# When the second and third groups' embedding gathers may be issued in a recommendation tower on one core

## The reference

```python
e = jnp.stack([tbl_0[ids[:, 0]], ..., tbl_38[ids[:, 38]]], axis=1)      # 512 x 39 x 16
# three layers, W of 128 x (39 * fields before); each one:
Xi = einsum('hjk,bjd,bkd->bhd', W.reshape(H, 39, Fi), X0, Xi) + b
res.append(Xi.sum(axis=2))                                              # 512 x 128
z = concatenate(res, axis=1)                                            # 512 x 384
h = relu(concatenate([z, dense_ctx]) @ W_top1 + b_top1)                 # 400 -> 512
h = relu(h @ W_top2 + b_top2)                                           # 512 -> 256
y = h @ W_top3                                                          # 512 x 1
```

## Time and profile before

| what | value |
|---|---|
| median of 3 executions | 723.21 us |
| lowest and highest of the 3 | 718.61 and 725.51 us |
| the profiled execution | 719.22 us |
| its span, first to last instruction | 716.8 us |
| mean granted TensorE clock in it | 0.981 |
| busy share of the span | PE 93%, DVE 82%, ACT 78%, POOL 49% |
| indirect DMAs of the whole kernel | 160, 955 ns each on POOL |

### The profile page before, as it was taken

One profiled execution on the slowest core, in us unless ns is written; L12 is line 12 of the kernel. 1 busy time (PEld: TensorE's weight loads), 2 busy tenths in 40 slices (PEclk: granted clock), 3 DMA queues, 4 the chain that ended last, 5 costly groups with the idle time before them and its releaser, 6 DMA issues.

```text
span 716.8 us, 11884 instructions
## 1 busy us (share of the span) xinstructions
PE 666.3 (93%) x2654; PEld 473.6 (66%) x2654; DVE 590.9 (82%) x956; ACT 558.5 (78%) x1939; POOL 347.9 (49%) x382
## 2 busy tenths in 40 slices
PE   3248899999999999999999999999999999999998
PEld 3135577777676767677767776677767777766653
DVE  3134789899998999899989998999989999999940
ACT  2114788988887888789878987998798888888842
POOL 7720388283747464655656474647464414002400
PEclk9759999999999999999999999999999999999999
DMA  8100561323223141414040504141414130200000
GB/s 274 17 7 9 111 169 24 71 47 67 51 60 59 37 80 26 88 17 102 11 103 9 109 8 105 12 105 12 104 14 101 13 99 6 75 1 1 0 1 0
DMA packets 66273, 39.51 MB, mean 55 GB/s; under 512 B 57558, under 2 KB 60630, under 8 KB 64084
## 3 DMA queue, kind: packets, MB, share of 16 engines
q1 hardware_dynamic: 59343, 37.58, 23.3%
q0 software_dynamic: 5120, 1.29, 2.0%
q10 hardware_dynamic: 1760, 0.15, 0.2%
HBM read 32.66 MB, written 2.40 MB: 49 GB/s over the span
## 4 chain that ended last, share of the span: by engine, by line
PE 75%; ACT 7%; issue 6%; DVE 5%; another core or an unknown queue 3%; DMA 3%; ACTq 0%; SPq 0%; POOL 0%; DVEq 0%; POOLq 0%
PE yb L913 17%; PE yb L914 16%; PE yb L915 16%; PE p L879 12%; ACT yb L571 5%; PE pq L890 4%; DVE acc L745 3%; DMA gram<-in_L_rec_W_dram 1%; PE yb L831 1%; PE p L989 1%; PE pq L844 1%; PE yb L1007 1%; DMA late<-x_scratch 1%; PE p L985 1%
## 5 line engine op out<-in xcount | busy, mean ns | idle before, releaser
L571 ACT ACTIVATE yb<-yb,x0t 128x128 f32<-128x128 f32 x1728 | 467.1, 379 | 78.6 <-PE yb L915 70.6
L745 DVE TENSOR_TENSOR acc<-acc,yb 128x512 f32<-128x512 f32 (+1 forms) x576 | 385.4, 669 | 40.5 <-ACT yb L571 9.1
L913 PE MATMUL yb<-w1h,x1h 128*128 128x512 f32 (+1 forms) x640 | 314.8, 492 | 6.9 <-DVE acc L745 4.0
L915 PE MATMUL yb<-w1h,x1l 128*128 128x512 f32 (+1 forms) x640 | 247.8, 387 | 0.0
L914 PE MATMUL yb<-w1l,x1h 128*128 128x512 f32 (+1 forms) x640 | 247.8, 387 | 0.0
L451 POOL TENSOR_TENSOR late<-late,x0r 117x512 f32<-117x512 f32 (+1 forms) x105 | 132.1, 1292 | 110.6 <-DMA late<-x_scratch 110.4
L913 PEld LDWEIGHTS yb<-w1h,x1h 128*128 128x128 f32 x640 | 120.0, 188 | 89.6 <-DVE acc L745 54.9
L400 POOL DMA_INDIRECT emb<-in_table_dram,idx x160 | 152.8, 955 | 43.0 <-issue 40.0
L914 PEld LDWEIGHTS yb<-w1l,x1h 128*128 128x128 f32 x640 | 120.8, 189 | 41.0 <-issue 24.8
L915 PEld LDWEIGHTS yb<-w1h,x1l 128*128 128x128 f32 x640 | 120.1, 188 | 24.7
L440 POOL TENSOR_TENSOR bdiag<-mask,x0t 128x312 f32<-128x312 f32 x64 | 45.5, 710 | 161.9 <-PE pq L890 158.5
(11 more groups left out here) (84 smaller groups left out, 327.2 us busy)
## 6 DMA issues: line engine op xcount, KB each, us to landing
late<-x_scratch SPq DMA_DIRECT2D x45, 312.0 KB
late<-x_scratch SPq DMA_DIRECT2D x30, 234.0 KB
emb<-in_table_dram,idx POOLq DMA_INDIRECT x160
gram<-in_L_rec_W_dram SPq DMA_DIRECT2D x1, 2496.0 KB
x_scratch<-x0r SPq DMA_DIRECT2D x15, 156.0 KB
late<-x_scratch SPq DMA_DIRECT2D x15, 156.0 KB
w2t<-in_L_rec_W_dram SPq DMA_DIRECT2D x1, 1280.0 KB
x0t<-embt SPq DMA_DIRECT2D x64, 20.0 KB
```

Source lines behind the costliest of these rows:

```text
L571: op = act.activation(part, part, ACT.Copy, scale=x0t[u][:, t, j:j + 1])
L745: dve.tensor_tensor(part, part, parts(y_bank(t, m), n), ALU.add).then_inc(summed, 1)
L913: pe.matmul(y[:, 0:w], hi, w1h[:, at:at + w], start=True, stop=False)
L915: pe.matmul(y[:, 0:w], lo, w1h[:, at:at + w], start=False, stop=True).then_inc(bank_ready, 1)
```

## The change

In the program of POOL every gather of group 1 first waits for `w_hi`. For gather i (0 to 9) the value is 2 + 10 - 10 + i + 1 = i + 3, so the first waits for ACT's first copy of W1 (n = 2), the sixth for its sixth, and the tenth for all 12 copies. No wait is written for group 2's gathers; they stand behind the tenth in the same queue. Nothing else differs.

```diff
                 rows_of(u, u)
                 pool.wait_ge(idx_ready, 2 * (u + 1))
                 for i in range(PER_Q):
+                    if u == 1:
+                        pool.wait_ge(w_hi, W0_BANKS + W_BANKS - PER_Q + i + 1)
                     gather(u, i)
             pool.wait_ge(embq_ready, 1)
             rows_of(2, 0)
```

## The result

The changed kernel takes 717.9 us (median of 20 executions, 714.95 to 720.19), the kernel before 722.8 us beside it (20 executions). The ratio is 0.9928, with a 95% interval of 0.9913 to 0.9942: 4.9 us faster, inside the 1% that the prediction called no change, and a third of the 14.6 us forecast. The profiled execution took 714.95 us with a span of 712.8, against 719.22 and 716.8 before.

What follows compares the result with a forecast made beforehand. The prediction took the opening to be bound by ACT's copies of W1, held up by gathers delaying PE's signals. Copies 17.0 us sooner, less 2.4 for group 2's run, gave 14.6 us: 708.6 us from 723.2, range 702 to 727.

Steps and rivals of the forecast that it cites:

- What bounds the kernel: Opening: bound by ACT's copies of W1, waiting 24.1 us because a long unbroken run of gathers holds back PE's signals.
- the gathers are not the cause: Rival on the opening: PE's signal is late for another reason, no change, 723.2 us; chance 0.15.
- The copies: ACT's copies of W1: sixth begins at 25.6, last ends at 30.8 instead of 47.79, 17.0 us sooner.
- That group 1 and group 2 would be there in time: Gathered rows: group 1 there by 37, wanted at 41.6; group 2 there by 51, wanted at 58.7.
- Group 2's run beside the first layer: First layer of group 0, 36 to 48 us: group 2's ten gathers delay PE's signals, costing 2.4 us.
- the upper bound: First layer: signals held until 4.2 us after the last gather, opening ends at 61.7, leaving 3.0 us of gain.
- The prediction's own signs: Opening: waits for remote in a first-layer stage over 11.4 us show a moved stall; line 554 after 55 refutes the forecast.
- the stall moves: Rival on the first layer: group 2's run holds its signals as the weights' were held, 720.2 us; chance 0.15.
- every gather arms the stall again: Rival on the copies of W1: one gather holds each next signal about 8.4 us, 735.1 us; chance 0.16, including otherwise slower.

Runs made afterwards that it cites:

- e1: The changed kernel without group 2's ten gathers in the opening (group 2 computed from group 0's rows): 703.0 us, 0.972 of the kernel before.
- e17: The changed kernel itself, unaltered, timed a third time in the fifth session: 717.3 us against 720.3 for the kernel before, 0.996.
- e3: The changed kernel with all ten gathers of group 1 waiting for the last of ACT's copies of W1: 720.1 us, 0.997 of the kernel before.
- e16: The changed kernel with both groups' gathers in later runs of five, and ACT's use of group 2 moved to slot (1, 2): 708.6 us, 0.979.
- e2: The changed kernel with group 2's ten gathers behind group 0's first layer, and ACT's use of them at slot (1, 5): 707.0 us, 0.979.
- e5: The changed kernel with group 2's gathers replaced by ten plain DMAs from POOL, second session: 695.7 us against 697.6 for the kernel before.
- e8: The changed kernel with group 2's gathers in runs of 3, 4 and 3, used at slot (1, 5), second session: 701.4 us against 697.6 before.
- e10: The changed kernel itself, unaltered, run again in the third session: 718.2 us against 723.4 for the kernel before, 0.993.
- e15: The kernel before with one wait: all of group 2's gathers behind ACT's last copy of W1, group 1 unpaced: 716.6 us, 0.990.
- e9: The changed kernel with group 2's gathers in two runs of five, behind ACT's copy of the turned fields and behind the opening's end: 704.5 us, 0.975.
- e18: The changed kernel with group 2's gathers in two runs of five, timed again in the fifth session: 701.9 us against 720.3 before, 0.972.
- e14: The changed kernel with a POOL multiplication between each two of group 2's ten gathers, in a session with holds: 704.8 us, 0.974.
- e13: The changed kernel with group 2's gathers replaced by thirty plain DMAs from POOL: 701.3 us, 0.969 of the kernel before.
- e11: The changed kernel with group 2's gathers replaced by ten plain DMAs from POOL, in a session with holds: 701.1 us, 0.971.
- e12: The changed kernel with group 2's gathers left out and twenty plain DMAs from SP's queue, in a session with holds: 702.2 us, 0.971.
- e4: The changed kernel with ten POOL multiplications of 128x480 elements in place of group 2's gathers: 701.6 us, 0.971 of the kernel before.

## Why the prediction was wrong

**What bounds the kernel: right.** ACT was waiting for PE's signals, and the gathers held them: leaving ten gathers out or slowing them freed the signals, and nothing that was put in their place held them again. One detail was off. The first of the four waits of the earlier trace rows, 6.99 us, holds the 1.69 us in which ACT itself issued its two small DMAs; the chain in the earlier trace rows has 5.25 for it. The rival "the gathers are not the cause" falls with e1. The rule that spoke for it, in the Trainium skill, "SBUF — State Buffer", "Who interferes with whom", that PE and ACT wait on nobody, is about memory ports. It does not speak against this case: in 36 to 45 us of the changed kernel's profile PE, DVE and ACT do nothing and the DMA engines are busy for 0.08 of the time, and e1 takes 15.0 us off that opening by leaving gathers out.

**The copies: the size right, the path partly luck.** Forecast 17.0 us, measured 19.8. The sixth copy began at 25.60, the very number of the working, but not as its mechanism had it, 2.1 us after POOL fell silent at 23.53. The fourth and fifth copies, taken over unchanged from 18.49 and 19.95, came at 20.73 and 22.87, so gathers 3 and 4 waited too and POOL fell silent at 24.68. From 23.86 to 25.55 ACT issued its two small DMAs, and the sixth copy followed 0.05 us later with the signal already there. In e17, the same kernel, the DMAs ended at 22.74 and the sixth copy began at 24.47, 0.9 us after POOL's last gather (23.57); the last copy ended at 30.00. The size of the gain holds (17.8 us there); that the two numbers agreed to a tenth is luck. That group 1 and group 2 would be there in time was right.

**Group 2's run beside the first layer: the step that failed.** The prediction took 2.4 us for this term, from the waits of 1.59 and 0.86 us ahead of the fourth and fifth copies. Measured, it is 15.0 us (e1 against the changed kernel's profile): 13.2 us of held signal and 1.8 us at PE's lower clock behind it, a term that the sum did not have. The mechanism was that of the upper bound: the signal was held until 3.1 us after the last gather (the bound had 4.2), and then the whole stage followed. The prediction's own signs for it came: the end of the opening later than 55 us, and a wait for "remote" in the first layer's stage. Without group 2's gathers (e1) the opening ends 64.73 - 45.39 = 19.34 us sooner than before, and with them 60.38 - 45.39 = 14.99 of these are lost again, which leaves 4.35 us; the profiled execution became 4.3 us shorter and the median 4.9. That is near the 3.0 of the rival "the stall moves", which had 0.15 and should have had most of the weight; it would have been lower still had the copies not gained 2.8 us more than forecast.

The reason was a wrong reading of two rows. That PE's signals had passed beside group 0's ten gathers, I took as a count: the effect sets in after about ten. e3 and e16 have it after four or five, e2 after some seven. And the waits of 1.59 and 0.86 us were its beginning: in e5, where nothing was held, the third to fifth copies began at 16.23, 17.08 and 17.94. The first ten may be a different case. In the kernel before the DMA engines had moved 118 packets of POOL's queue by 14 us, where the eighth gather was being issued; a gather is 32 packets (5,120 for 160), so that is less than four of them, while the loads of the weights (q1) took 77% of the same engines' time (packets, MB, share of the 16 engines, 0 to 14 us):

```profile
q1 hardware_dynamic: 638, 4.06, 77.0%
q0 software_dynamic: 118, 0.03, 2.1%
```

That this is why they held nothing before 16 us is argued only, and where nothing was held at all the numbers were about the same (111 to 116 packets by 14 us in e5 to e8). And with the onset read as ten, the fifteen gathers from 26 us on would still have passed it at 38 us, in the middle of the first layer: the working had all it needed to put the hold there, and I priced it by two short waits of a stage in which the hold had only begun.

**The size.** 14.6 us were forecast and 4.9 measured. Two terms of the sum were off and one was missing: 19.8 instead of 17.0 for the copies, 13.2 instead of 2.4 for the held signals, and 1.8 instead of nothing for the clock. The first hid a part of the others.

**The rival "every gather arms the stall again"** was wrong in size. In the changed kernel's profile the last five copies followed each other without a wait from 25.60 on, with gathers issued among them from 26.46; e10 shows the same from 27.16. In e17 the sixth, seventh and eighth copies began at 24.47, 25.91 and 28.28 with a gather between each two, intervals of 1.4 and 2.4 us where the rival needed more than 5.4.

## What to carry to other kernels

When a wait is moved out of the way of a burst, ask where the burst goes: it is a cost of the burst and its neighbour, not of the place. Price the new place by the mechanism that the old one showed at full strength, not by its first symptoms. Check an agreement in one number against the row that released it: here the forecast start of a copy was met because another instruction ended there. Here the cure was to cut the burst (two runs of five at pauses that the program has anyway, 2.5 to 2.8% against 0.4 to 0.7%) and not to move it. And a kernel with unbroken indirect DMAs should be timed in more than one session: this one changed by 25 us where no line of it changed.

## What the runs showed of the hardware

- Indirect DMAs issued from POOL 1.25 us apart delayed PE's semaphore signals once four to seven of a run were out. The signals then came through one at a time, 5.6 to 9.1 us apart (before, e3, e15), and the last held one 0.8 to 3.4 us after the run ended (e2, e15; 2.1 in the kernel before, 3.1 in the changed one). The delay adds up: the eighth bank of W1 was turned by 20.49 in the kernel before, and ACT copied it at 44.70.
- Runs of four or five delayed nothing that shows in e9, e18 and the loop; in e16 one delayed a signal by 2.0 us. Gathers 2.2 us apart delayed one by 1.5 us (e14). Thirty plain DMAs from POOL, 0.53 us apart (e13), ten of them (e11), twenty from SP (e12) and 10.6 us of POOL's arithmetic (e4) delayed nothing.
- PE that had stood idle from 35.22 ran at a granted clock of 0.50 from 48 to 53 us, and the first layer took 12.05 us there instead of 10.27.
- Only PE's signals were seen late. In the kernel before, in the middle of the run, DVE followed ACT's copy (27.90 + 0.60 = 28.50) at 28.60 and PE followed DVE at 29.34, 0.05 us after its end:

```profile
28.60 0.69 DVE L698 TENSOR_TENSOR w1l<-yb,w1h 128x512 fp32r<-128x512 f32 x1 [7.25 <-remote]
```

```profile
29.34 1.12 PE L831 MATMUL yb<-ident,w2t 128*128 128x128 f32 x4 [7.29 <-issue]
```

- In one session of five the kernel before took 697.6 us, and the four kernels traced beside it showed none of it. What sets that stays open, as does the path that the signals and the gathers share. The ends of matmuls in the profile are modelled, so no row tells a late signal from a late end of PE's writing. And every execution here has a recorded span of its own, so whether the signals are late when nothing is recorded is not known either.
